# A two-layer transformer kernel on one core: score products on four row groups at once, shorter operand stacks, and no full-array products ahead of the transposed scores

## What is computed

```
x  = encodings                                    # 8 x 512 x 128
xn = layernorm(x)
x  = x + L0_attn(xn) + L0_ffn(xn)                 # 16 heads of 8; ffn 128 -> 512 -> 128, block-quantized, gelu
xn = layernorm(x)
x  = x + L1_attn(xn) + L1_ffn(xn)                 # 16 heads of 8, causal; 8 experts, each silu(x wg) * (x wu) @ wd, summed
```

## Time and profile before

| | us |
|---|---|
| median of 3 runs | 1633.93 (1624.28 to 1640.37) |
| the profiled execution | 1633.84 |
| its span | 1632.1 |
| mean granted TensorE clock | 0.914 of full speed |

### The profile page before, as it was taken

The page is one execution under the profiler, slowest core; times in us unless marked ns, Lnnn a source line. Parts: engine busy times, 40 slices in busy tenths (PEclk is TensorE's granted clock), DMA queues, the critical chain, the costliest instruction groups (busy, mean ns, idle before and its releaser), DMA issues. The chain is left out here.

```text
span 1632.1 us, 23537 instructions
## 1 busy us (share of the span) xinstructions
PE 1501.3 (92%) x8440; PEld 840.4 (51%) x8440; DVE 1036.6 (64%) x2379; ACT 823.3 (50%) x1220; POOL 678.2 (42%) x791
## 2 busy tenths in 40 slices
PE   2899999999999999369999999999999999999987
PEld 1444444444444443245656656666666566666655
DVE  3545655565655453157876767777777677777743
ACT  2335455555545445135655556555655565555650
POOL 4222324243333223245554455454545554545440
PEclk9559888898979789679999999999999999999997
DMA  3312223232413221231010110111111101111003
GB/s 118 85 35 74 73 82 93 68 98 71 125 56 106 79 64 61 72 92 54 28 52 27 31 47 28 34 48 36 32 53 32 43 28 35 32 37 32 18 14 111
DMA packets 59025, 93.95 MB, mean 58 GB/s; under 512 B 12119, under 2 KB 22876, under 8 KB 56862
## 3 DMA queue, kind: packets, MB, share of 16 engines
q1 hardware_dynamic: 57902, 92.00, 18.9%
q10 hardware_dynamic: 1008, 0.46, 0.1%
HBM read 50.08 MB, written 40.11 MB: 55 GB/s over the span
## 5 line engine op out<-in xcount | busy, mean ns | idle before, releaser
L1133 POOL TENSOR_TENSOR a_h_lo<-a_h,a_h_hi 128x512 fp32r<-128x512 f32 x256 | 329.2, 1286 | 143.6 <-ACT a_h_hi L1180 134.2
L668 DVE TENSOR_REDUCE l_mx<-bank_pair 128x2 f32<-128x1024 f32 (+1 forms) x192 | 200.0, 1044 | 237.7 <-PE bank_pair L886 236.5
L1241 DVE SCALAR_TENSOR_TENSOR a_h<-a_h,bank_pair 128x512 f32<-128x512 f32 x256 | 175.6, 686 | 171.9 <-ACT a_h L1176 169.0
L749 ACT ACTIVATE l_E<-bank_pair 128x1024 f32<-128x1024 f32 (+1 forms) x192 | 169.3, 883 | 179.3 <-PE bank_pair L139 178.8
L192 POOL TENSOR_SCALAR_AFFINE_SELECT l_E<-l_E 128x256 f32<-128x256 f32 (+1 forms) x192 | 95.6, 500 | 382.0 <-ACT l_E L749 382.0
L1187 ACT ACTIVATE a_E<-bank_pair 128x1024 f32<-128x1024 f32 (+1 forms) x192 | 169.8, 884 | 166.5 <-PE bank_pair L139 166.3
L168 DVE CUSTOM_DVE_ANT_0 bank_pair<-bank_pair,mask 128x512 f32<-128x512 f32 (+3 forms) x512 | 238.0, 516 | 7.1 <-PE bank_pair L129 6.9
L1180 ACT ACTIVATE a_h_hi<-a_h 128x512 fp32r<-128x512 f32 x256 | 160.6, 627 | 115.5 <-DVE a_h L1247 115.5
L192 POOL TENSOR_SCALAR_AFFINE_SELECT a_E<-a_E 128x256 f32<-128x256 f32 (+1 forms) x192 | 95.0, 495 | 281.6 <-ACT a_E L1187 281.5
L1247 DVE TENSOR_TENSOR a_h<-a_h,bank 128x512 f32<-128x512 f32 x256 | 176.0, 688 | 27.0 <-DVE a_h L1241 0.5
L1176 ACT ACTIVATE a_h<-bank_pair 128x512 f32<-128x512 f32 x256 | 151.6, 592 | 72.8 <-PE bank_pair L1319 69.2
(11 more groups left out here) (134 smaller groups left out, 2379.1 us busy)
## 6 DMA issues: line engine op xcount, KB each, us to landing
st<-stack_d SPq DMA_DIRECT2D x112, 128.0 KB, 3.1
st<-stack_d SPq DMA_DIRECT2D x224, 64.0 KB, 3.0
stack_d<-l_q_k_hi SPq DMA_DIRECT2D x48, 256.0 KB
stack_d<-l_q_k_lo SPq DMA_DIRECT2D x32, 256.0 KB
o_d<-l_O SPq DMA_DIRECT2D x32, 256.0 KB, 2.0
o_d<-a_O SPq DMA_DIRECT2D x32, 256.0 KB, 2.0
l_st<-stack_d SPq DMA_DIRECT2D x16, 128.0 KB, 3.6
l_st<-stack_d SPq DMA_DIRECT2D x32, 64.0 KB, 3.5
```

The source lines that it names most:

```text
L668: nc.vector.tensor_reduce(out, src, AX.X, ALU.max).then_inc(S_used, 1)
L749: nc.scalar.activation(E[:, pair % SLOTS_E, at_col:at_col + HALVES * w].rearrange("p (r c) -> p r c", r=HALVES), pair_of("T", g, n)[:, :, ...
L1133: nc.gpsimd.tensor_tensor(h_lo[:, q % RH, :], h[:, q % RH, :], h_hi[:, q % RH, :].bitcast(F32), ALU.subtract).then_inc(h_lo_ready, 1)
L1241: nc.vector.scalar_tensor_tensor(hq, hq, 1.0, g_bank[:, :], ALU.add, ALU.mult).then_inc(silu_ready, 1)
```

## The change

It touches both blocks, and its parts are:

1. A stack has 24 rows of q and k (three slots; the product of the two low parts is left out) and 4 rows of maxima, 28 in all. It fits in 32 rows, so one 128-row tile holds two quads: quad g stands at rows 64 r + 32 (g % 2). There are two tiles, that is four stacks, in both blocks. A stack comes in with two DMAs instead of six. Stores to DRAM are six a projection instead of five.
2. S(g+1, n) and T lie on different row groups now, and are issued together: `scores_and_keys(g, n)` waits for the banks of both, then issues the products in the order S half 0, S half 1, T half 0, T half 1. In layer 0 T belongs to the same g and n (all six T of a quad in one step), where it was spread over two quads; in the expert block it is T(g, n-1), in the cells where it was.
3. `keep_warm` is not called any more: 384 products of 512 columns are gone. The mask products of S units 4 and 5 are two of 256 columns instead of four of 128.
4. M is a fp32r product with a fp32r identity, of 8 columns instead of 72.
5. In layer 0 the feed-forward of a tile runs one quad behind its attention instead of three ahead, the quantization of the weights and `sel_setup` come later, the first weights have their own semaphore (`w0_in`), `turn_input(0, a)` and `queries(1, ...)` come behind step 5, and PV(g) ends the same quad.

```diff
-SLOTS = 4
+SLOTS = 3
...
+def row_of(g, r):
+    return HALF * r + GROUP * (g % STACKS_A_BUFFER)
+def buffer_of(stacks, g):
+    return stacks[g // STACKS_A_BUFFER % len(stacks)]
...
             def T(g, n):
-                if n == 0:
-                    pe.wait_ge(mrow_in, MAX_LOADS * (g + 1))
-                begin("T", g, n)
-                keep_warm(nc, pair_of("T", g, n), identb, mask)
-                keys_by_queries(nc, pair_of("T", g, n), st[g % STACKS], n % 3, n // 3).then_inc(T_ready, 1)
...
+            def scores_and_keys(g, n):
+                more, here = in_range(g + 1), in_range(g)
+                if more:
+                    if n == 0:
+                        pe.wait_ge(stack_in[(g + 1) % STACKS], STACK_LOADS * ((g + 1) // STACKS + 1))
...
+                    begin("S", g + 1, n)
+                if here:
+                    if n == 0:
+                        pe.wait_ge(mrow_in, MAX_LOADS * (g + 1))
+                    begin("T", g, n)
...
+                for k in range(2):
+                    for r in range(HALVES):
+                        if more and k < len(score_blocks):
+                            scores(nc, pair_of("S", g + 1, n)[:, r, :], stacks, g + 1, r, score_blocks[k], k == 0, False)
+                    for r in range(HALVES):
+                        if here and k < len(key_blocks):
+                            ins = keys_by_queries(nc, pair_of("T", g, n)[:, r, :], stacks, g, r, n // 3, key_blocks[k])
...
+                if more:
...
+                        ins = nc.tensor.matmul(diagonal, identb[:, :], part, start=False, stop=True)
+                    ins.then_inc(S_ready, 1)
...
             def tile_of(g):
-                return g + 3 if 0 <= g + 3 < NT * B else None
+                return g - 1 if 0 <= g - 1 < NT * B else None
...
+            def scores_and_keys(g, n, m):          # of the expert block
+                more, here = n is not None and in_range(g + 1), m is not None and in_range(g)
...
+                        if m == 0:
+                            pe.wait_ge(mrow_in, MAX_LOADS * (g + 1))
+                        if g > 0 or m > 0:
+                            pe.wait_ge(exp_done, UNITS_A_QUAD * g + m)
...
+                    c = NC * odd + n
+                    scores_and_keys(g, c if c < UNITS_A_QUAD else None, c - 1 if 0 < c <= UNITS_A_QUAD else None)
```

More of the change, by code:

```diff
@@ L121, in spread, with scores, keys_by_queries @@
     return nc.tensor.matmul(bank[:, :], sel[rows, b % 2, :], rden[rows, :], start=True, stop=True)
[L124 to L141, removed]
+def scores(nc, bank, stacks, g, r, block, first, last):
+    j, t, col = block
+    w, st, rows = P * (t + 1), buffer_of(stacks, g), slice(row_of(g, r), row_of(g, r) + SLOT_ROWS)
+    return nc.tensor.matmul(bank[:, col:col + w], st[rows, j, 0, bass.ts(t, P)], st[rows, j, 1, 0:w], start=first, stop=last)
+def keys_by_queries(nc, bank, stacks, g, r, j, block):
+    kb, col = block
+    w, st, rows = width(kb), buffer_of(stacks, g), slice(row_of(g, r), row_of(g, r) + ROWS)
+    return nc.tensor.matmul(bank[:, col:col + w], st[rows, j, 1, bass.ts(kb, P)], st[rows, j, 0, N - w:N], start=True, stop=True)
 def keep_warm(nc, pair, identb, mask):
@@ L236, in put, with scores_and_keys @@
                 order.append(unit)
-        def scores_of(n):
+        def scores_and_keys(n):
             put(("S", g + 1, n), 0 <= g + 1 < QUADS)
[L241 to L245, removed]
+            put(("T", g, n), 0 <= g < QUADS)
+        scores_and_keys(0)
         put(("V", 0, b + 1), u == 0 and 0 <= b + 1 < B)
@@ L543, in _ @@
                 if in_range(g):
-                    causal(g, 1)
-                    causal(g, 2)
+                    for n in range(2, UNITS_A_QUAD):
+                        causal(g, n)
                 if u == 0 and ok(y2):
@@ L885, in S @@
                     for r in range(HALVES):
-                        ins = nc.tensor.matmul(pair[:, r, at_col + w - P:at_col + w], identb[:, :], mask[:, N - P:N], start=False, stop=True)
-                ins.then_inc(S_ready, 1)
+                        if here and k < len(key_blocks):
+                            ins = keys_by_queries(nc, pair_of("T", g, n)[:, r, :], stacks, g, r, n // 3, key_blocks[k])
+                            if r == HALVES - 1 and k == len(key_blocks) - 1:
+                                ins.then_inc(T_ready, 1)
@@ L925, in queries @@
             def queries(layer, b):
+                if layer == 0 and b == 0:
+                    pe.wait_ge(w0_in, 16 * FIRST_LOADS)
                 pe.wait_ge(xnT_ready[layer], b + 1)
@@ L934, in values @@
             def values(layer, b):
+                if layer == 0 and b == 0:
+                    pe.wait_ge(w_in, 16 * SMALL_LOADS)
                 begin("V", layer, b)
@@ L1008, in _ @@
                     queries(0, a)
-                if more:
-                    S(g + 1, 1)
-                if back:
-                    T(g - 1, 4)
+                scores_and_keys(g, 1)
                 if u == 1 and ok(y2):
```

325 lines of the change are left out of this document (149 added, 176 removed).

## The result

| | before | after |
|---|---|---|
| median of 4 runs on one chip, us | 1633.41 | 1662.63 (1658.44 to 1666.11) |
| ratio, 95% interval | | 1.0181 [1.0125, 1.0237] |
| span of the profiled execution | 1632.1 | 1661.0 |

The change makes the kernel 1.8% slower. The forecast was 1621 us, 0.8% faster; the range held the time, the direction was wrong. What came is nearly what rival 2 had (1658).

What follows compares the result with a forecast made beforehand. PE was taken to set the pace in both blocks. From 1633.8 us, layer 0 +45, expert block -42, start -12 and drain -4 gave 1621 us, range 1570 to 1672 (the forecast's own 1600 to 1645).

Steps and rivals of the forecast that it cites:

- rival 2: Layer 0: PE and DVE alternate at half clock without refund, 21.6 us a quad, +82 us, total 1658; chance 0.25.
- the refund for the clock: Layer 0: full clock from PV until the second step behind it takes quads from 21.6 to 20.4 us; +45 us.
- My sum at half clock without refund: Layer 0: base quad 18.8 us plus 2.8 us of other PE work, 21.6 us a quad.
- In the turn: Layer 0, from quad to quad: PV 4.16 us at half clock; refund about 0.4 us, down to the DMA's 4.3.
- In the steps: Layer 0: 1.20 us a step at half clock besides DVE's reads, 0.80 at full; refund 0.8 us a quad.
- The mechanism: Layer 0: step n cannot start before DVE has read S of step n-1, so PE and DVE alternate.
- The reading of the clock: Layer 0: the score mix with `keep_warm` does not raise the clock, PV does; removing `keep_warm` frees 3.1 to 5.9 us a quad.
- Expert block: Merged S and T save 1.8 us a quad, 0.5 given back, 1.3 x 32 = 42 us saved.
- DVE's price: Expert block: DVE 1.4 us late in cell 6, the gate bank absorbs 0.9; 0.5 us a quad given back.
- The extra 0.07 us a step: Both blocks: a merged 512-column step costs some 0.07 us more than a pair, 22 us over ten steps a quad.
- rival 4: Both blocks: four row groups overlap, but not wholly; 22 us more, total 1643; chance 0.09.
- Drain: Between the blocks: a short piece of T and four DMA issues fewer ahead of the first expert weights, 4 us saved.

Runs made afterwards that it cites:

- run 1: Changed kernel with T one step later in layer 0, T(g, n-1) beside S(g+1, n): 1571.78 us, 0.9654 of the kernel before.
- run 4: Changed kernel with layer 0's S and T unmerged, T's bank wait behind S's products and signal: 1567.10 us, 0.9632 of the kernel before.
- Run 9: Changed kernel with only T put ahead of S in the list of units: 1599.39 us, 0.9787 of the kernel before.
- Run 2: Changed kernel with the two full-array products (`keep_warm`) ahead of each T of layer 0 put back: 1786.75 us, 1.0978 of the kernel before.
- run 5: Kernel before, its own expert block, without its full-array products (`keep_warm`): 1674.99 us, 1.0244 of the kernel before.
- run 3: Changed kernel with T one step later and the two full-array products put back: 1534.33 us, 0.9442 of the kernel before.
- run 10: As run 3, with layer-1 transposes moved behind step 2 and the maxima's transfer issued ahead of the reciprocals': 1506.55 us, 0.9227 of the kernel before.
- run 11: As run 10, with one full-array product ahead of each T instead of two: 1580.65 us, 0.9674 of the kernel before.

## Why the prediction went wrong

**The step that failed** is the refund for the clock: "full from somewhere in PV until the second step behind it. That refunds about 0.4 us where PV's end is then limited by the DMA's 4.3, and 0.8 in the steps: 20.4 us a quad." Worked out from the starts of DVE's reads over 20 late quads of the changed kernel, the four quads of a batch take 23.6, 23.4, 20.0 and 19.7 us, 86.7 together. My sum at half clock without refund was 4 x 21.6 = 86.4; with it 81.6. So the sum without refund was right to 0.3 us. That it fits so closely is partly luck, for it had half clock throughout, and the clock was full for 208 of the 659 us. The clock itself behaved as forecast (0.66 measured, below 0.75 expected), but gave almost nothing back:

- *In the turn.* PV took 3.0 to 4.2 us (means of the four kinds of quads) instead of 4.16, but behind its end PE waited up to 1.5 us for the transfer. From M to the first product behind PV 4.7 to 5.9 us pass, 5.0 in the mean, where the sum had 4.7 without the refund and 4.3, taken from the earlier trace rows, with it. In runs 1 and 4, where the first products behind PV do not wait for the maxima of T, PE goes on at PV's end.
- *In the steps.* From the end of one read to the start of the next I had 1.20 us at half clock. In the quads with the least other work it is 1.06, 0.91 and 1.07 behind the first three reads (the clock's gain) and 1.52 and 1.41 behind the next two, where S has two planes and the mask products 256 columns: 417.99 + 0.96 to 420.46 above. I gave 0.2 us a quad for that; it is 0.5, and with it some 0.2 of the 0.8 are left.

The turn is 0.7 us above the forecast and the steps 0.6: 20.4 + 1.3 = 21.7 a quad, as measured (86.7 / 4). So layer 0 costs 82 us more, what rival 2 had for it, 31 x 3.0 - 11. The rest follows from the table: 1632.1 - 15.6 + 81.8 + 5.2 - 42.5 - 0.1 = 1660.9.

**The mechanism was right.** That PE and DVE alternate through the `begin` waits, each step waiting for the read of the one before, was the core of the working, and runs 1, 4 and 9 show it three ways: move T, move T's wait, or swap two units in the list, and 91, 96 and 63 us go, at a clock that hardly changes (0.67, 0.67 and 0.68 against 0.66). Run 9 leaves least room for another cause: its products and their order are those of the changed kernel. Run 2 shows it from the other side.

**The reading of the clock was half wrong, though the sum took no gain from it.** I wrote that the mix around the scores does not raise the clock and PV does, from a stretch at half clock with the products in it, and costed their removal as 3.1 to 5.9 us a quad of freed time. That does not follow: the products mostly do not raise the clock in the kernel before, but they hold it, and run 5 shows that their removal alone costs 43 us in layer 0. Of the 82 us one cannot give 43 to the clock and the rest to the waits, since the waits alone keep the clock low (run 2); but without the alternation the products are worth 37 us (run 3 against 1).

**The other terms.**

- *Expert block:* -42.5 against -42, of which a part is luck. The quads that nothing disturbs went from 26.6 to 25.4 us and from 27.3 to 26.4, some 33 us in 31 quads; most of the rest is three quads of 30.1 to 32.4 us in the kernel before, in which PE waited 1.9 to 2.9 us for the maxima's transfer, and the changed block took 798 to 808 us in the other runs. DVE's price came too, but in another place: PE waits 8.2 us for silu where it waited 7.0 before, and in cell 5, where S's second half waits for DVE with T behind it, the step takes 1.03 us instead of the 0.74 of S and T apart.
- *Row groups.* The extra 0.07 us a step, which the prediction drew from the 3.07 of the Trainium skill (TensorE: Matmul & The Clock Gate, Part 3, Measured speedup vs the span model), is not seen, since a merged step costs what a pair did, and rival 4 falls. Taken plainly, 0.43 x (4 / 3.07 - 1) would have been 0.13; the 0.07 is half of that, with no reason given. Nor do show two halves "for the price of one": a pair takes 0.43 us, and a full-array product of as many columns 0.23 (1036.22 to 1036.45), so a pair costs hardly less than two products in turn. No run times a product on one row group alone.
- *Start:* -15.6 against -12.
- *Drain:* +5.2 against -4. I had counted the issues saved ahead of the expert weights (the first stack load to the first S is 1.2 us shorter) and not the six stores a projection instead of five, which add 1.2 us in each of two projections. But 3.8 us of the difference lie ahead of the first of these stores, and what makes them is open.
- *The first two batches:* 14 us less instead of 11.

What stays open: which part of runs 1 and 3 ScalarE's exponentials still cost, since no run takes them away; and which property of the full-array products holds the clock, their rows or the time that they fill.

## What to carry to other kernels

When two units share one issue slot and both bank waits stand ahead of both, ask of the rotating banks whose read each wait is for: if it is that of the step before, the engine pair alternates, and a change that takes 96 us off PE's busy time loses 82. Put one unit a step later, or its wait behind the other's products, before anything is merged. Credit a faster clock only to work that nothing else ends: in a loop that waits for another engine in each step it buys idle time. And before filler products are taken out, ask not only whether the clock rises in them but whether it stays up because of them.

## What the runs showed of the hardware

Where PE hardly waits, the full-array products decided the clock (0.85 with them and 0.67 without, run 5), and busy time does not show it. PE was busy for 92% of layer 0 in run 5 (572.79 of 619.70) at a clock of 0.67, and for 96% at 0.85 with the products; in run 10 87% went with 0.93. The Trainium skill (TensorE: Matmul & The Clock Gate, Part 1, What's actually happening) says that the clock follows how busy PE has been; by the busy share of the profile these runs do not agree, so that share is no guide to it where most products use 24 to 36 rows. Nor does the fall need a long wait: in run 5 the clock fell 29 times in layer 0, and ahead of 27 of these falls PE had no single gap of 1 us or more in the last 8 us.

The dose matters: with two products of 512 columns ahead of each T the clock was 0.93 (run 10), with one 0.70 (run 11), with none 0.67 (run 1, two waits more). Removing the second product cost 74 us.

Four row groups with products of two kinds at once cost no more than two: 0.43 us at full clock, as the pair did, and 0.74 at half for 512 columns, where the pair took 0.72.
